# Softplus of a selective-scan mixer: where its operations stand among sixteen units, and which engine does them

## The reference

```python
h = _L0_tok_ref(...)                                   # kernel matrix of a state space model, 512 features
h = concatenate([cls_tok, h])
h = h + _L0_attn_ref(_layernorm(h), ...)               # the mixer: the change is here
h = h + _L0_ffn_ref(_layernorm(h), ...)                # 32 experts, top 4
h = h + _L1_attn_ref(_layernorm(h), ...)
h = h + _L1_ffn_ref(_layernorm(h), ...)
```

```python
xn = x * rsqrt(mean(x*x) + EPS) * norm_w
x_inner, z = split(xn @ in_proj_w.T)
xc = silu(conv1d(x_inner, 4 taps) + conv_b)
x_ssm = xc @ x_proj_w.T                                # 33 columns: B (16), C (16), one for dt
dt = softplus(x_ssm[..., -1:] * dt_w + dt_b)
h = exp(dt * A) * h + (dt * u) * B                     # a recurrence over t, for each e and n
y = sum(h * C, n) + D * u
out = (y * silu(z)) @ out_proj_w.T + x
```

## Time and profile before

| | |
|---|---|
| median of 3 runs | 3083.64 us (3079.12 to 3083.67) |
| profiled execution | 3080.41 us, of which the span is 3078.8 us |
| mixer's first `bu` to its last scan's end | about 510 to 1712 us of the span |
| busy over the whole span | PE 2499.6, DVE 1969.0, ACT 1386.3, POOL 1234.7 us |
| six turns of the mixer, 738.70 to 1197.70 us | 459.00 us: DVE busy 427.83, PE 378.57, ACT 349.62, POOL 299.32 |

### The profile page before, as it was taken

How to read it: one execution, slowest core, us unless ns; L and a number is a source line. 1 busy time by engine, 2 the same in 40 slices (tenths; PEclk the granted TensorE clock), 3 DMA queues, 4 the chain that set the end, 5 groups by cost and what they waited for, 6 DMA issues and landing times. The chain is left out here.

```text
span 3078.8 us, 47872 instructions
## 1 busy us (share of the span) xinstructions
PE 2499.6 (81%) x17070; PEld 2118.1 (69%) x17071; DVE 1969.0 (64%) x2723; ACT 1386.3 (45%) x3353; POOL 1234.7 (40%) x758
## 2 busy tenths in 40 slices
PE   5999996788888888888887760399999679999986
PEld 4999996788788887877876540144444357787875
DVE  7566325999999999999999452022222256677653
ACT  0332426777777777777777120011111123333432
POOL 3100003666666666666666106400000244554331
PEclk9988978899999999999999875699999887899996
DMA  5700000000000000000000006455755321111000
GB/s 208 302 1 1 1 1 29 29 29 30 29 30 29 30 29 30 29 30 29 29 29 29 7 0 199 125 187 170 245 171 181 101 59 29 51 49 31 8 8 14
DMA packets 63511, 201.49 MB, mean 65 GB/s; under 512 B 12346, under 2 KB 17594, under 8 KB 60474
## 3 DMA queue, kind: packets, MB, share of 16 engines
q1 hardware_dynamic: 25210, 96.31, 9.1%
q0 software_dynamic: 26272, 80.77, 8.2%
q10 hardware_dynamic: 11808, 21.50, 1.8%
HBM read 130.31 MB, written 68.23 MB: 64 GB/s over the span
## 5 line engine op out<-in xcount | busy, mean ns | idle before, releaser
L837 POOL TENSOR_TENSOR m_hs<-m_hs,m_BC 128x1040 f32<-128x1040 f32 x256 | 616.4, 2408 | 335.7 <-DVE m_hs L945 335.7
L757 ACT ACTIVATE m_dA<-m_dt,m_A 128x128 f32<-128x128 f32 x2048 | 616.2, 388 | 270.7 <-DVE m_hs L945 151.7
L636 PE MATMUL m_py<-m_hs,ident 128*128 128x130 f32 x4096 | 566.6, 297 | 165.8 <-POOL m_hs L837 165.7
L636 PEld LDWEIGHTS m_py<-m_hs,ident 128*128 128x128 f32 x4096 | 532.7, 209 | 185.3 <-POOL m_hs L837 182.9
L945 DVE TENSOR_TENSOR_SCAN m_hs<-m_dA,m_own 128x1040 f32<-128x1040 f32 x256 | 593.5, 2318 | 25.8 <-DVE m_own L934 16.1
L934 DVE TENSOR_TENSOR m_own<-m_BC,m_own 128x1040 f32<-128x1040 f32 x256 | 317.9, 1242 | 11.6 <-DVE m_hs L945 4.6
L588 PE MATMUL m_pw<-m_xg,m_w_in 128*128 128x130 f32 x2048 | 259.9, 285 | 46.0 <-DVE m_xc L898 34.8
L588 PEld LDWEIGHTS m_pw<-m_xg,m_w_in 128*128 128x128 f32 x2048 | 249.8, 200 | 51.3 <-DVE m_xc L898 40.0
L1376 PE MATMUL e_pG<-e_w_gu,e_xT 128*128 x656 | 235.6, 503 | 11.1 <-issue 7.2
L1356 POOL DMA_DIRECT2D e_x<-slots x80 | 43.1, 538 | 403.8 <-PE e_pX L1367 397.0
L1376 PEld LDWEIGHTS e_pG<-e_w_gu,e_xT 128*128 128x128 f32 x656 | 119.8, 192 | 91.7 <-issue 25.7
(11 more groups left out here) (274 smaller groups left out, 4602.8 us busy)
## 6 DMA issues: line engine op xcount, KB each, us to landing
m_BC<-xs SPq DMA_DIRECT2D x16, 2080.0 KB, 9.1
slots<-a_zero POOLq DMA_DIRECT2D x48, 512.0 KB, 39.1
e_w_gu<-in_gate_up_w SPq DMA_DIRECT2D x32, 768.0 KB, 5.0
e_x<-slots POOLq DMA_DIRECT2D x82, 256.0 KB, 3.0
slots<-e_y ACTq DMA_DIRECT2D x82, 256.0 KB, 2.5
e_w_d<-in_down_w SPq DMA_DIRECT2D x32, 256.0 KB, 5.6
out_h<-t_ho SPq DMA_DIRECT2D x8, 520.0 KB, 3.3
a_AT<-in_A_cols SPq DMA_DIRECT2D x8, 512.0 KB, 7.3
```

What stands on the lines that cost most here:

```text
L636: mm = pe.matmul(py[k % 2][:, 0:MT], ident[:, :], hs[u % NB][:, n, :], start=False, stop=(half == 1 and n == HN - 1))
L757: act.activation(images(dA[u % NB][:, n, :])[:, :, 1:TOK], images(dt[b][:, k, :])[:, :, 1:TOK], ACT.Exp, scale=A[:, at:at + 1]).then_inc(d ...
L837: pool.tensor_tensor(hs[u % NB][:, :, :], hs[u % NB][:, :, :], BC[b][:, ST + half * HN:ST + (half + 1) * HN, :], ALU.mult).then_inc(prod_r ...
```

## The change

The softplus is begun a unit earlier on ACT, loses one operation on POOL, and is spread wider there.

- ACT: `take_xs` at 10, `steps` at 11 (before: 11 and 12). `steps` takes |x| in 8 pieces straight from PSUM. The 1 is taken off e1 by ACT (Identity with bias -1, into `lp`), and Ln writes `e1` in place. relu(x) is a function of its own, `relus`, 8 pieces from PSUM into `dt` behind unit 12
- POOL: `log_step` has three steps behind units 10, 12 and 14: ex - lp, added to the logarithm, added to `dt`. The last is split in two, the first tile (130 columns) and the other seven (910), each of which sets `dt_ready`
- `residual` moves from units 13 and 14 (for g + 2) to units 1 and 3 of the next turn (for its g + 1)
- ACT and DVE wait for the first part of dt ahead of tile 0 and for the second ahead of tile 1
- DVE: `conv_piece` behind odd units, and `add_tiles` behind unit 11, now stand between `bu` and the scan of that unit; the next turn's first `du` comes behind unit 15 (before: 14)

```diff
-TAP_AT, SILU_AT, TAKE_AT, STEP_AT = 5, 9, 11, 12
-LOG_AT = 9
-MEAN_OF, VAR_OF, SQUARE_AT, RESID_AT, SCALE_AT = 0, 2, 8, 13, 13
+TAP_AT, SILU_AT, TAKE_AT, STEP_AT = 5, 9, 10, 11
+LOG_AT = (10, 12, 14)
+MEAN_OF, VAR_OF, SQUARE_AT, RESID_AT, SCALE_AT = 0, 2, 8, (1, 3), 13
...
-                    if j == 1:
-                        pe.wait_ge(x_ready, q * ET)
+                        pe.wait_ge(relu_ready, q * ET)
...
-            def steps(q, b, first=False):
+            def steps(q, first=False):
 
                 act.wait_ge(s_done, q + 1)
+                if not first:
+
+                    act.wait_ge(dt_ready, q * 2)
                 for e in range(ET):
-                    act.activation(dt[b][:, e, :], pw[1][:, 0:MT], ACT.Identity, bias=dt_b[:, e:e + 1],
-                                   scale=dt_w[:, e:e + 1]).then_inc(x_ready, 1)
-                act.wait_ge(x_ready, (q + 1) * ET)
-                if not first:
-
-                    act.wait_ge(dt_ready, q)
-                act.activation(ex[:, :, :], dt[b][:, :, :], ACT.Abs).then_inc(ln_steps, 1)
-                act.wait_ge(ln_steps, q * 5 + 1)
+                    act.activation(ex[:, e, :], pw[1][:, 0:MT], ACT.Abs, bias=dt_b[:, e:e + 1],
+                                   scale=dt_w[:, e:e + 1]).then_inc(abs_ready, 1)
+                act.wait_ge(abs_ready, (q + 1) * ET)
                 act.activation(ex[:, :, :], ex[:, :, :], ACT.Exp, scale=-1.0).then_inc(ln_steps, 1)
...
-                act.activation(dt[b][:, :, :], dt[b][:, :, :], ACT.Relu).then_inc(ln_steps, 1)
-                act.wait_ge(ln_steps, q * 5 + 3)
-                act.activation(lp[:, :, :], e1[:, :, :], ACT.Ln).then_inc(ln_steps, 1)
+                act.wait_ge(ln_steps, q * 4 + 2)
+                act.activation(lp[:, :, :], e1[:, :, :], ACT.Identity, bias=-1.0).then_inc(ln_steps, 1)
+                act.activation(e1[:, :, :], e1[:, :, :], ACT.Ln).then_inc(ln_steps, 1)
+
+            def relus(b):
+                for e in range(ET):
+                    act.activation(dt[b][:, e, :], pw[1][:, 0:MT], ACT.Relu, bias=dt_b[:, e:e + 1],
+                                   scale=dt_w[:, e:e + 1]).then_inc(relu_ready, 1)
...
-                act.wait_ge(dt_ready, g + 1)
                 for u in range(NU):
                     k, half = divmod(u, 2)
+                    if u == 0 or u == 2:
+                        act.wait_ge(dt_ready, g * 2 + 1 + k)
...
+                        if u == STEP_AT + 1:
+                            relus(1 - b)
...
                 if step == 0:
-                    pool.wait_ge(ln_steps, q * 5 + 5)
-                    pool.tensor_tensor(e1[:, :, :], e1[:, :, :], unit, ALU.subtract).then_inc(log_steps, 1)
+                    pool.wait_ge(ln_steps, q * 4 + 3)
+                    pool.tensor_tensor(ex[:, :, :], ex[:, :, :], lp[:, :, :], ALU.subtract).then_inc(log_steps, 1)
                 elif step == 1:
...
+                    pool.wait_ge(ln_steps, q * 4 + 4)
+                    pool.wait_ge(log_steps, q * 2 + 1)
+                    pool.tensor_tensor(e1[:, :, :], e1[:, :, :], ex[:, :, :], ALU.add).then_inc(log_steps, 1)
                 else:
-                    pool.wait_ge(log_steps, q * 3 + 3)
-                    pool.tensor_tensor(dt[b][:, :, :], dt[b][:, :, :], lp[:, :, :], ALU.add).then_inc(dt_ready, 1)
...
+                    pool.wait_ge(log_steps, q * 2 + 2)
+                    pool.wait_ge(relu_ready, (q + 1) * ET)
+                    for lo, hi in ((0, 1), (1, ET)):
+                        pool.tensor_tensor(dt[b][:, lo:hi, :], dt[b][:, lo:hi, :], e1[:, lo:hi, :], ALU.add).then_inc(dt_ready, 1)
...
-                    if not last and LOG_AT <= u < LOG_AT + 4:
-                        log_step(g + 1, 1 - b, u - LOG_AT)
-                    if more and RESID_AT <= u < RESID_AT + 2:
-                        residual(g + 2, u - RESID_AT)
+                    if not last and u in LOG_AT:
+                        log_step(g + 1, 1 - b, LOG_AT.index(u))
+                    if not first and not last and u in RESID_AT:
+                        residual(g + 1, RESID_AT.index(u))
...
+                    elif not last and CONV_AT <= u < CONV_AT + NP:
+                        conv_piece(g + 1, 1 - b, u - CONV_AT)
+                    elif not first and ADD_AT <= u < ADD_AT + 2:
+                        add_tiles(g - 1, u - ADD_AT)
                     dve.wait_ge(bu_ready, g * NU + u + 1)
...
-                    if half == 0:
-                        if k < ET - 1:
-                            step_input(g, b, k + 1)
-                        elif not last:
-                            step_input(g + 1, 1 - b, 0)
+                    if half == 0 and k + 1 < ET:
+                        step_input(g, b, k + 1)
+                    if u == NU - 1 and not last:
+                        step_input(g + 1, 1 - b, 0)
...
-                        if CONV_AT <= u < CONV_AT + NP:
+                        if CONV_AT <= u < CONV_AT + NP and half == 0:
                             conv_piece(g + 1, 1 - b, u - CONV_AT)
-                    if not first and ADD_AT <= u < ADD_AT + 2:
+                    if not first and ADD_AT <= u < ADD_AT + 2 and half == 0:
                         add_tiles(g - 1, u - ADD_AT)
```

More of the change, by code:

```diff
@@ L492, in mamba @@
         pick = sb("pick", [XP, P])
-        one = sb("one", [P, ET])
         xg = [sb(f"xg{i}", [P, FT, MT]) for i in range(2)]
@@ L523, in mamba @@
             sem, ("u_ready", "z_ready", "xs_done", "xs_ready", "xs_out", "BC_in", "s_done"))
-        x_ready, ln_steps, log_steps, dt_ready, du_ready = map(
-            sem, ("x_ready", "ln_steps", "log_steps", "dt_ready", "du_ready"))
+        abs_ready, relu_ready, ln_steps, log_steps, dt_ready, du_ready = map(
+            sem, ("abs_ready", "relu_ready", "ln_steps", "log_steps", "dt_ready", "du_ready"))
         dA_ready, bu_ready, scanned, prod_ready, summed = map(sem, ("dA_ready", "bu_ready", "scanned", "prod_ready", "summed"))
@@ L659, in _ @@
             x_proj(0, 0)
-            pe.wait_ge(pick_set, 3)
+            pe.wait_ge(pick_set, 2)
             spread_step(0)
@@ L739, in steps @@
                 act.activation(ex[:, :, :], ex[:, :, :], ACT.Exp, scale=-1.0).then_inc(ln_steps, 1)
-                act.wait_ge(ln_steps, q * 5 + 2)
+                act.wait_ge(ln_steps, q * 4 + 1)
                 act.activation(e1[:, :, :], ex[:, :, :], ACT.Identity, bias=1.0).then_inc(ln_steps, 1)
-                act.activation(dt[b][:, :, :], dt[b][:, :, :], ACT.Relu).then_inc(ln_steps, 1)
-                act.wait_ge(ln_steps, q * 5 + 3)
-                act.activation(lp[:, :, :], e1[:, :, :], ACT.Ln).then_inc(ln_steps, 1)
+                act.wait_ge(ln_steps, q * 4 + 2)
@@ L769, in turn @@
                         if u == STEP_AT:
-                            steps(g + 1, 1 - b)
+                            steps(g + 1)
                             if more:
@@ L787, in _ @@
             root(1)
-            steps(0, 0, first=True)
+            steps(0, first=True)
+            relus(0)
             turn(0, 0, first=True)
@@ L798, in _ @@
         def _(pool):
-            unit = one[:, :].unsqueeze(2).broadcast_to([P, ET, MT])
             pool.memset(pick[:, :], 0.0).then_inc(pick_set, 1)
-            pool.memset(one[:, :], 1.0).then_inc(pick_set, 1)
-            pool.wait_ge(pick_set, 2)
+            pool.wait_ge(pick_set, 1)
             pool.memset(pick[2 * ST:XP, :], 1.0).then_inc(pick_set, 1)
@@ L819, in log_step, with turn @@
                 if step == 0:
-                    pool.wait_ge(ln_steps, q * 5 + 5)
-                    pool.tensor_tensor(e1[:, :, :], e1[:, :, :], unit, ALU.subtract).then_inc(log_steps, 1)
+                    pool.wait_ge(ln_steps, q * 4 + 3)
+                    pool.tensor_tensor(ex[:, :, :], ex[:, :, :], lp[:, :, :], ALU.subtract).then_inc(log_steps, 1)
                 elif step == 1:
[L823 to L827, removed]
-                else:
-                    pool.wait_ge(log_steps, q * 3 + 3)
-                    pool.tensor_tensor(dt[b][:, :, :], dt[b][:, :, :], lp[:, :, :], ALU.add).then_inc(dt_ready, 1)
-            def turn(g, b, last=False, more=True):
+                    pool.wait_ge(ln_steps, q * 4 + 4)
+                    pool.wait_ge(log_steps, q * 2 + 1)
+                    pool.tensor_tensor(e1[:, :, :], e1[:, :, :], ex[:, :, :], ALU.add).then_inc(log_steps, 1)
+                else:
+                    pool.wait_ge(log_steps, q * 2 + 2)
+                    pool.wait_ge(relu_ready, (q + 1) * ET)
+                    for lo, hi in ((0, 1), (1, ET)):
+                        pool.tensor_tensor(dt[b][:, lo:hi, :], dt[b][:, lo:hi, :], e1[:, lo:hi, :], ALU.add).then_inc(dt_ready, 1)
+            def turn(g, b, first=False, last=False):
                 pool.wait_ge(BC_in, (g + 1) * 16)
@@ L838, in turn @@
```

(21 more changed lines are left out.)

## The result

| | before | changed |
|---|---|---|
| median | 3081.38 us (3079.02 to 3083.67, 4 runs) | 3007.06 us (3006.09 to 3008.87, 4 runs) |
| span of the profiled execution | 3078.8 us | 3006.4 us |

The ratio of the changed kernel's time to that of the kernel before is 0.976, with a 95% interval of 0.9743 to 0.9776: 74 us faster, where 67 from the profiled execution (3013) and a median of 3015 had been forecast. In the spans the difference is 72.4 us. The first scan begins at 505.76 instead of 512.19 us, which is 6.4 us; from there to the last add into hT behind the mixer (1654.06 instead of 1724.44) are 64.0 us less; the remaining 2.0 us lie in stages that the change doesn't touch.

A forecast was written before the change was run, and what follows sets the result against it. DVE sets the pace in the mixer turns. New stalls of 2.9 us a turn replace 7.0; 4.1 saved over 15 turns plus 5.9 ahead of turn 0 is 67.4, so 3080.4 becomes 3013.0, median 3015, range 2992 to 3045.

The forecast's parts named there:

- A stall of two-operand DVE rows behind POOL: `du` stands until POOL's operation ends; unit 12's stall goes (up to 2.2 us), 1.1 to 1.2 us a turn comes at unit 15.
- ACT's chain: From `steps` to the next exponentials 10.7 us; DVE newly waits 0.3 us at unit 12 and 1.2 at unit 13.
- the 0.2 us for a late y: At `scale_x`: blocked again where y is late and scan 13 ends ahead of POOL's second step; 0.2 us a turn added.
- PE: At unit 12, waits for y shrink from 1.6 to 0.8 us a turn and overlap with ACT's lateness.
- `residual`: Behind unit 2, product and moved residual take 3.6 us, so `du` finds POOL idle by about 0.2 us.
- The turn's head: Start of next turn: dt's first tile is about 2.2 us ahead of the first product; first convolution tap waits 0.3 us.
- DVE's order: Units 3, 5 and 11: work between product and scan covers a 0.2 us gap, gaining 0.1 us each, 0.3 a turn.
- the 1.5 us: DVE's new wait a turn for ACT's exponentials at units 12 and 13, with scan 5 ending 1.5 us later.
- Ahead of turn 0: Before the first turn, the first scan starts at about 506.2 us against some 512.1: 5.9 us saved.
- the one in which PE's queue stays the limit: At unit 12 the y wait keeps 1.6 to 2.6 us; saving 2.1 us a turn, about 3043 us; chance 0.13.
- The slower one, PE at the lower clock: Output projection at 1.2 GHz each turn, y at unit 12 later by 6.5 us; about 3100 us; chance 0.04.
- the second rival: ACT not late at units 12 and 13, DVE ahead of POOL's second part; 2976 to 2980, half 2995; chance 0.12.

The follow-up runs named there:

- The experiments with `relus`: On the changed kernel, `relus` on ACT stands behind unit 13 instead of 12: 2999.44 us, ratio 0.9744 to the kernel before.
- with the convolution: On the changed kernel, DVE's convolution pieces and `add_tiles` stand behind their scans again: 2994.81 us, ratio 0.973 to the kernel before.
- the experiments, 24 to 27 us: Changed kernel with POOL's last step behind unit 13 and convolution pieces and `add_tiles` behind their scans: 0.9671; the same with that step in one piece: 0.9683.

## Why the prediction was right

The mechanism was the forecast one: the standing time and the waits that were to go went, and the new waits came at the units that were named. Point by point, forecast against measured a turn:

- *A stall of two-operand DVE rows behind POOL.* `du` at unit 12 fell to 0.28 us. The part at unit 15 was forecast at 1.15 and is (19.6 - 48 x 0.277) / 6 = 1.05 us. Moving POOL's step alone took it away (0.9705). The old stalls of 7.0 us less the new ones of 1.05 and 1.56 give 4.4, and the six turns are shorter by 4.4 us each.
- *ACT's chain.* 0.3 us at unit 12 and 1.2 at unit 13 were forecast; the rows have 0.31 and 1.25. The step from the first |x| to the next exponentials is 773.05 - 762.26 = 10.8 us against 10.7. The experiments with `relus` and with the convolution took this wait away, and both found the next one behind it, `scale_x` at POOL's second step. That this second limit lay so near was in the forecast only as the 0.2 us for a late y.
- *PE.* y no longer waits in these turns, where up to 0.8 us overlapping with ACT's wait had been allowed. The clause went by the old durations of the sum and the projection, 3.83 and 6.56 us; with a wait of 0.5 us ahead of them they take 2.06 and 5.53. The 0.2 us added for it were not spent: `scale_x` takes 0.68 us.
- *`residual`.* `du` behind unit 2 was to find POOL idle by about 0.2 us. The operation ends at 802.49 + 1.20 = 803.69 and `du` starts at 803.86 and takes 0.28 us.
- *The turn's head.* 0.3 us ahead of the first convolution piece was forecast; it is 0.4 us in six turns, so under 0.1 a turn. In every second turn DVE stands about 1 us at the jump of the loop (0.97 us ahead of 1153.11), which by my reading gives ACT that much more time; I had left this out. POOL's last step was put at 0.3 + 2.1 us and takes 2.54, as its first part is 0.46 us and not 0.3.
- *DVE's order.* Of the 0.3 us that it was to win less than 0.1 can be found. What it costs through ACT was counted in the 1.5 us; its undoing gave back 9 us in all.
- *Ahead of turn 0.* 5.9 us forecast, 6.4 measured; `relus` at 498.64 follows the logarithm without a table load. The Trainium skill (ScalarE: Activation LUTs, Table sets: the hidden batching unit) has relu in every set; the trace agrees for the set of the logarithm.

The sum of the terms was 4.1 us a turn; it is 64.0 / 15 = 4.3. Of the miss of 5 us in the span, 2.5 are in the turns, 0.5 ahead of turn 0 and 2.0 in stages that the forecast left alone, of which no run says why. That the sum came so close is luck in part: the forecast gain of DVE's order was 0.2 us a turn too high, and the stalls forecast for a late y and for the turn's head were 0.2 each too high, which works the other way.

Of the rivals, the one in which PE's queue stays the limit did not happen, but its mechanism is real: with ACT a unit later it is back, at 21 us. The slower one, PE at the lower clock, had no sign of it: the granted clock rose from 0.93 to 0.96. That the changed kernel's own added waits could be taken out (the second rival) was shown by the experiments, 24 to 27 us, though not in the way that it named.

What each part is worth: ACT a unit earlier and POOL's steps a unit later 47 us alone, on the kernel before; ACT's earlier start 21, taken back from the changed kernel; the operation moved from POOL to ACT 11; the move of `residual` nothing; the split of the last step 32 to 38 where it stands, nothing that can be told a unit earlier; DVE's order minus 9. These don't add up to 74, since each was measured with the others either all in or all out.

## What to carry to other kernels

When a short row of VectorE has a mean well over its median, look at what GpSimd runs at those times: the standing time counts as busy and no wait names it. GpSimd work is then best placed by where VectorE's two-operand rows fall, and counted by the gap between them. If such a row depends on a GpSimd operation itself, it should have been released before the last operation runs and not by its end, or the next GpSimd operation, if one stands ready, gets in first. And before work is put ahead of the bound engine's main operation, look at who waits for that operation's end: here a start 1.5 us earlier for ACT was worth 0.6 us a turn more than the covered gaps of 0.1 to 0.2 us.

## What the runs showed of the hardware

A VectorE row of two SBUF operands that is already waiting when a GpSimd operation ends went next (1.34 us, ahead of product 15 in the changed kernel, 1.33 to 1.50 in all 15 turns). One that is released by the end of that operation came after the next one (2.46 to 2.48 us with the last step whole, in all 15 turns). Where GpSimd had nothing ready behind the step, ahead of turn 0 of that kernel, the row took 0.30 us. The Trainium skill (SBUF — State Buffer, Who interferes with whom) says that issue order decides who blocks. The trace agrees: the row that started ahead of product 15 took 1.34 us, and the one that started behind it 2.48. What costs twice is a release by the operation's own end.

GpSimd's 130 columns take a row of 0.459 us and 910 columns 2.116, but the two together last 2.54 us, as they overlap by some 0.04: 0.15 us more than 2.39 for the 1040 in one. So the split cost 0.15 us here. A fixed part of that size in every operation does not fit the rows of 520 and 1040 columns (1.20 and 2.39 us); why the short row takes 0.16 us more than an eighth of 1040 columns stays open.
